# Per-head values laid out by DMA from rows in DRAM, in a fused attention and mixture-of-experts block

## The chip, the cores and the metric

The kernel runs on one core of a Trainium2 chip. The metric is the device time of one execution in microseconds, as the median of several runs. Before the change it is 536.37 us, the median of three runs (535.66, 536.37 and 537.6).

## The reference

For 4 batches of 1024 tokens of 128 features, the block normalises the tokens, runs a 16-head attention (4 heads see all earlier tokens, 12 only the last 32 and themselves) and a mixture of 16 experts of which 4 are chosen per token, and multiplies the two.

```
xn = layernorm(x)
q, k, v = split(xn @ w_qkv + b_qkv)               # 16 heads of 8 features
ctx_g = attend(q, k, v of heads 0..3,  j <= i)
ctx_l = attend(q, k, v of heads 4..15, i - 32 <= j <= i)
s = concat(ctx_g, ctx_l) @ w_out + b_out
g = silu(xn + experts(xn) + shared(xn))           # 4 of 16 experts per token, 64 wide
out = x + s * g
```

## The kernel before, in words

**Sections and order.** The work is a list of steps, walked by every engine in the same order: a first section (weights, and the preparation of batch 0), a body that is walked three times (the attention and experts of batch b, and woven into them the preparation of batch b + 1), and a last section. The order is written out by hand as strings of letters, `FIRST_ORDER`, `BODY_ORDER` and `LAST_ORDER`; `woven` takes the next step of the stream that each letter names: R the attention run, A the maxima and operands of the next heads, X the experts, P the preparation (layer norm, q, k, the first maxima), T the routing, V the values, C, 0 and 1 the context and the two output halves. Each engine's queue is strictly in this order, and a step that waits holds everything behind it on that engine. There are eight PSUM banks; two rings of three banks each (ATT, EXP) are dealt out in the order of the steps.

**Attention.** The heads come in four groups of four; groups 0, 1 and 2 of the order are local, group 3 is global. Queries and keys are kept as three half-precision planes in DRAM. For each group, SP loads strips (`qtmp`, `kall`, `("strips", g)`) and pads (`qpad`, `kpad`, `("pads", g, half)`, `("kpads", g)`), in which each of the four heads has its own 32 partitions and its own columns. `("max", g, n)` are products of `qpad` and `kall` that give each row's maximum, `("qfull", g, c)` takes the maximum off the queries and leaves them in `qall` (ACT), `("score", g, n)` are the scores, exponentiated by ACT into `prob`, and `("pv", g, n)` multiplies them with the values. SP issues the strips of group 1 only after the qall of group 0 has been copied.

**Values of the local heads.** A pv product of a local group takes as weights `vbd[:, j, group, :]`: for the block j of 32 tokens, the 128 partitions are (head, token in block), and of the 32 value columns a head's partitions hold only that head's own 8, with zeros elsewhere (the other 32 columns are the mask itself, for the sums). `("vn", c)` computes the values of 512 tokens as rows (tokens on partitions). ACT casts the local columns to the fast 32-bit format (`vn_hi`), DVE takes the rest (`vn_lo`), and four steps `("v", c, i)` multiply both with a 0/1 tile `repeat` (lines 639 and 640), which copies the 32 tokens of block i of each tile to all four heads. DVE evicts each result through a mask, `vmask`, into `vbd` (helper `tt`, line 964, called under `kind == "v"`). The global heads' values go straight to `vg` (ACT).

**Experts.** `("up", c, t)` is seven products (three for the gate, three for up, one that spreads the routing weight), then ACT, POOL (`wrow`, `hid`) and DVE, and `("down", c, t)` one product into bank 7. `("outT", c)` transposes an output half, DVE adds it to `xres`, and SP stores it.

**SP's queue around a change of batch** holds, in this order, the stores of the two output halves, the load of the next input (`xin`), the load of `xres` (which waits until both stores have landed), then strips and pads of group 1, 2 and 3.

## Time and profile before

| | before |
|---|---|
| median of 3 runs | 536.37 us |
| the profiled execution | 535.39 us, of which its span is 533.6 |
| PE matmul | 479.1 us busy, 90% of the span, 3832 instructions |
| DVE | 347.8 us, 65%, 755 instructions |
| ACT | 329.1 us, 62% |
| POOL | 269.0 us, 50% |
| SP's DMA queue | 143696 packets, 31.41 MB, 30.4% of 16 engines' span |
| mean granted TensorE clock | 0.988 |

The profile is of one execution. Durations of matmuls overlap, since they are pipelined, so that the distance between two starts is what one costs PE. "Releaser" in a wait is the instruction that ended it. An idle engine costs nothing unless it is on the chain of waits.

### The profile page before, as it was taken

The page shows a single profiled execution, that of the slowest core. Times are in us where ns is not written, and L with a number is a line of the kernel's source. Part 1 is how long each engine was busy: PE and PEld are TensorE (multiplying, and loading weights), DVE is VectorE, ACT ScalarE, POOL GpSimd, SP SyncE. Part 2 cuts the span into 40 slices and gives each one's busy share as a digit, 9 for nine tenths or more (in the row PEclk, how much of TensorE's full clock was granted, in tenths as well). Part 3 has the DMA queues.
Part 4 walks back from the last instruction along what each step waited for, and adds up shares of the span by engine and source line. Part 5 has one row for each costly group of instructions (what it writes and reads, how often), then busy time and mean ns, then how long its engine had stood idle before and what let it go on. Part 6 is the DMA issues. An engine that isn't in the chain of part 4 may idle for free.

```text
span 533.6 us, 10570 instructions
## 1 busy us (share of the span) xinstructions
PE 479.1 (90%) x3832; PEld 286.6 (54%) x3832; DVE 347.8 (65%) x755; ACT 329.1 (62%) x654; POOL 269.0 (50%) x239
## 2 busy tenths in 40 slices
PE   1859978899999989899999988999999998989995
PEld 0647554555446755555446765545546765544442
DVE  7876439775977638776787546776788532676414
ACT  3536753767956554666957556475976566366972
POOL 3407942265737852254655872145664963016623
PEclk9979999999999999999999999999999999899998
DMA  9275374000450575000350387000170178000001
GB/s 214 79 177 100 57 99 66 1 1 2 121 77 1 164 97 78 1 1 1 116 83 1 93 153 94 2 1 1 32 159 9 40 125 133 4 2 0 1 1 39
DMA packets 144077, 32.37 MB, mean 61 GB/s; under 512 B 120966, under 2 KB 136346, under 8 KB 144026
## 3 DMA queue, kind: packets, MB, share of 16 engines
q1 hardware_dynamic: 143696, 31.41, 30.4%
q8 instruction: 30, 0.49, 0.4%
q10 hardware_dynamic: 330, 0.30, 0.3%
q14 instruction: 21, 0.17, 0.1%
HBM read 22.25 MB, written 9.44 MB: 59 GB/s over the span
## 4 chain that ended last, share of the span: by engine, by line
PE 56%; DVE 13%; ACT 8%; issue 7%; SPq 6%; POOL 3%; DMA 3%; DVEq 2%; POOLq 1%; ACTq 0%
PE bank L791 8%; PE bank L739 6%; PE bank L708 5%; PE bank L678 5%; PE bank L572 4%; SPq L536 4%; PE bank L574 4%; PE bank L573 4%; PE bank L755 3%; ACT stage L936 2%; DVE mxp L1176 2%; DMA kall<-planes 2%; PE bank L646 2%; PE bank L779 2%; PE bank L715 2%
## 5 line engine op out<-in xcount | busy, mean ns | idle before, releaser
L936 ACT ACTIVATE stage<-bank 128x512 f32<-128x512 f32 (+3 forms) x240 | 112.7, 539 | 59.2 <-PE bank L712 27.9
L1253 POOL TENSOR_TENSOR wrow<-wrow,gates 128x512 f32<-128x512 f32 x64 | 82.5, 1289 | 90.6 <-ACT wrow L865 90.0
L1176 DVE TENSOR_REDUCE mxp<-bank 128x1 f32<-128x512 f32 (+4 forms) x192 | 89.8, 516 | 23.7 <-PE bank L681 14.2
L1262 POOL TENSOR_TENSOR hid<-hid,wrow 128x512 f32<-128x512 f32 x64 | 82.4, 1287 | 28.4 <-DVE hid L1140 23.5
L1245 POOL TENSOR_TENSOR maxd<-mxp,k 128x512 f16<-128x512 f32 x32 | 34.7, 1083 | 95.9 <-DVE mxp L1178 51.2
L791 PE MATMUL bank<-hid,down_w 128*128 128x512 f32 x144 | 76.0, 618 | 0.0
L1140 DVE SCALAR_TENSOR_TENSOR hid<-hid,bank 128x512 f32<-128x512 f32 x72 | 48.7, 677 | 39.5 <-PE bank L574 28.6
L854 ACT ACTIVATE hid<-bank 128x512 f32<-128x512 f32 x72 | 43.7, 606 | 44.2 <-PE bank L574 44.2
L1178 DVE TENSOR_REDUCE mxp<-bank 128x8 f32<-128x512 f32 x48 | 30.9, 686 | 49.3 <-PE bank L690 49.0
L678 PE MATMUL bank<-kall,qpad 128*128 128x512 f16 (+4 forms) x192 | 52.2, 320 | 10.6 <-DVE mxp L1176 3.7
L572 PE MATMUL bank<-xh,up_hi 128*128 128x512 f32 x144 | 58.7, 408 | 2.0 <-DVE hid L1140 1.2
L708 PE MATMUL bank<-kpad,kall 128*128 128x512 f16 (+3 forms) x192 | 55.2, 330 | 4.7 <-ACT stage L936 2.4
L574 PE MATMUL bank<-xl,up_hi 128*128 128x512 f32 x144 | 56.8, 394 | 0.0
L573 PE MATMUL bank<-xh,up_lo 128*128 128x512 f32 x144 | 56.5, 393 | 0.0
L859 ACT ACTIVATE gates<-bank 128x512 f32<-128x512 f32 x72 | 43.6, 605 | 5.8 <-POOL wrow L1253 5.8
L708 PEld LDWEIGHTS bank<-kpad,kall 128*128 128x128 f16 x192 | 17.9, 97 | 54.3 <-issue 21.5
L739 PE MATMUL bank<-stage,vg 128*32 128x512 f32 (+3 forms) x384 | 40.7, 498 | 0.0
L865 ACT ACTIVATE wrow<-bank 128x512 f32<-128x512 f32 x64 | 39.4, 616 | 0.3 <-PE bank L779 0.3
L678 PEld LDWEIGHTS bank<-kall,qpad 128*128 128x128 f16 x192 | 17.1, 97 | 37.4 <-DVE mxp L1176 16.1
L929 ACT ACTIVATE qall<-bank 128x512 f16<-128x512 f32 x32 | 18.3, 600 | 25.7 <-PE bank L663 25.6
L779 PE MATMUL bank<-cwT,pairsel 128*128 128x512 f32 x64 | 33.9, 529 | 0.3 <-issue 0.2
L572 PEld LDWEIGHTS bank<-xh,up_hi 128*128 128x128 f32 x144 | 27.1, 188 | 10.5 <-DVE hid L1140 2.5
(158 smaller groups left out, 907.7 us busy)
## 6 DMA issues: line engine op xcount, KB each, us to landing
planes<-qkh SPq DMA_DIRECT2D x16, 256.0 KB, 3.2
qtmp<-planes SPq DMA_DIRECT2D x16, 256.0 KB, 3.2
kall<-planes SPq DMA_DIRECT2D x16, 256.0 KB, 3.5
qpad<-planes SPq DMA_DIRECT2D x128, 32.0 KB, 2.8
kpad<-planes SPq DMA_DIRECT2D x48, 64.0 KB, 3.3
xin<-in_L_attn_x_dram SPq DMA_DIRECT2D x4, 512.0 KB, 4.5
planes<-qkl SPq DMA_DIRECT2D x8, 256.0 KB, 3.4
xres<-in_L_attn_x_dram SPq DMA_DIRECT2D x4, 512.0 KB, 3.7
```

The costliest lines, as they stand in the source:

```text
L572: pe.matmul(ps[:], w_hi, x_hi, start=True, stop=False)
L573: pe.matmul(ps[:], w_lo, x_hi, start=False, stop=False)
L574: return pe.matmul(ps[:], w_hi, x_lo, start=False, stop=True)
L678: ins = pe.matmul(ps[:, 0:cols], qpad[:, j, :, :], kall[:, g % 2, CH * c:CH * c + cols], start=True, stop=not last, skip_group_check=True)
L708: ins = pe.matmul(ps[:, 0:cols], kall[:, g % 2, P * j:P * (j + 1)], kpad[:, g % 2, q0 // BLK:(q0 + cols) // BLK, h, :], start=True, stop=n ...
L739: ins = pe.matmul(acc[BLK * h:BLK * (h + 1), q0 - CH * c:q0 - CH * c + cols], vg[:, j, h, :], prob[:, (SCORES_BEFORE[g] + m) % NPROB, 0:cols],
L791: pe.matmul(banks[Y][:], down_w[:, t, :], hid[:, i % NHID, :], start=(t == 0), stop=(t == NUP - 1)).then_inc(down_done, 1)
L936: act.activation(prob[:, t % NPROB, 0:cols], ps[:, 0:cols], ACT.Exp).then_inc(freed, 1)
L1140: dve.scalar_tensor_tensor(out=hid[:, i % NHID, :], in0=hid[:, i % NHID, :], scalar=1.0, in1=banks[at.bank(up)][:], op0=ALU.add, op1=ALU.m ...
L1176: ins = dve.tensor_reduce(mxp[:, c, j:j + 1], ps[:, 0:cols], AX_X, ALU.max)
L1253: pool.tensor_tensor(row, row, gates[:], ALU.mult).then_inc(gated, 1)
L1262: pool.tensor_tensor(hid[:, i % NHID, :], hid[:, i % NHID, :], wrow[:, (EP * c + t) % NWT, :] if t < EP else gates[:], ALU.mult)\
```

## The change

`vbd` is no longer computed with products. `("vn", c)` is evicted by ACT as plain 32-bit rows into a tile `vn`; SP stores these rows in a DRAM tensor `v_rows` (1024 tokens by 96 columns, two stores of 128 x 4 x 96). A single step `("v", 0)` per batch then issues twelve loads, one for each of the three local groups and four heads, which write the head's 8 columns of 32 blocks of 32 tokens to that head's 32 partitions of `vbd`. The zeros around them are written once, by POOL in the first section. The tiles `repeat`, `vn_hi` and `vn_lo`, the spreading products, the split and the masked evictions are gone. PE waits for `v_loaded` before the first pv product of a batch. The three order strings are new.

```diff
-    return [step for c in range(NCH) for step in [("vn", c)] + [("v", c, i) for i in range(4)]]
+    return [("vn", c) for c in range(NCH)] + [("v", 0)]
...
+                    elif kind == "vn":
+                        c = s[1]
+                        sp.wait_ge(emptied[at.bank(s)], at.taken(s))
+                        if at.next:
+                            sp.wait_ge(v_loaded, 16 * 4 * GLOBAL * at.next)
+                        sp.dma_start(v_rows.rearrange("(t p) d -> p t d", p=P)[:, TPC * c:TPC * (c + 1), :],
+                                     vn[:, TPC * c:TPC * (c + 1), :]).then_inc(v_stored, 16)
+                    elif kind == "v":
+                        if at.section is FIRST:
+                            sp.wait_ge(v_zeroed, 1)
+                        else:
+                            sp.wait_ge(pv_done, b * SCORES_BEFORE[HG] + SCORES_BEFORE[GLOBAL])
+                        sp.wait_ge(v_stored, 16 * NCH * (at.next + 1))
+                        for g in range(GLOBAL):
+                            for h in range(4):
+                                own = slice(HD * h, HD * (h + 1))
+                                sp.dma_start(vbd[BLK * h:BLK * (h + 1), :, g, own],
+                                             v_rows[:, BLK * g:BLK * (g + 1)][:, own].rearrange("(j k) d -> k j d", k=BLK))                                    .then_inc(v_loaded, 16)
...
-                        pe.matmul(used, repeat[:, i, :], vn_hi[:].rearrange("p t d -> p (t d)"), start=True, stop=False)
-                        done(at, s, pe.matmul(used, repeat[:, i, :], vn_lo[:].rearrange("p t d -> p (t d)"), start=False, stop=True))
...
+                        if g == 0 and n == 1:
+                            pe.wait_ge(v_loaded, 16 * 4 * GLOBAL * (b + 1))
...
-                            act.activation(vn_hi[:], tile[:, :, BLK:D], ACT.Copy)
+                            if at.next:
+                                act.wait_ge(v_stored, 16 * NCH * at.next)
+                            act.activation(vn[:, TPC * s[1]:TPC * (s[1] + 1), :], tile[:, :, BLK:D], ACT.Copy)
...
-                        elif kind == "v":
-                            c, i = s[1], s[2]
-                            tt(vbd[:].rearrange("p (t i) g c -> p i t g c", i=4)[:, i, TPC * c:TPC * (c + 1), :, 0:BLK],
-                               ps[:, 0:TPC * GLOBAL * BLK].rearrange("p (j g c) -> p j g c", j=TPC, g=GLOBAL),
-                               vmask[:, 0:GLOBAL].unsqueeze(1).broadcast_to([P, TPC, GLOBAL, BLK]), ALU.mult).then_inc(freed, 1)
...
+                    pool.memset(vbd[:, :, :, 0:BLK].rearrange("p j g c -> p (j g) c"), 0.0).then_inc(v_zeroed, 1)
```

The order strings move instructions. On SP, at the change from one batch to the next, the kernel before has (a row is a run of equal issues; `out_dram<-xres` are the stores of the output halves):

```order
L536 DMA qpad<-planes 32x16x32 x8
L546 DMA kpad<-planes 32x32x32 x4
L552 DMA out_dram<-xres 128x4x128 x2
L506 DMA xin<-in_L_attn_x_dram 128x8x128
L510 DMA xres<-in_L_attn_x_dram 128x8x128
L526 DMA qtmp<-planes 128x1024
L526 DMA kall<-planes 128x1024
```

and after the change:

```order
L537 DMA qpad<-planes 32x16x32 x8
L547 DMA kpad<-planes 32x32x32 x4
L555 DMA v_rows<-vn 128x4x96 x2
L571 DMA out_dram<-xres 128x4x128
L566 DMA vbd<-v_rows 32x32x8 x12
L571 DMA out_dram<-xres 128x4x128
L507 DMA xin<-in_L_attn_x_dram 128x8x128
L511 DMA xres<-in_L_attn_x_dram 128x8x128
L527 DMA qtmp<-planes 128x1024
L527 DMA kall<-planes 128x1024
```

The two stores of rows and the twelve loads stand ahead of the second output store and of everything behind it.

On PE, from the transposes of the first output half on, the kernel before has, in the second body pass (L779 spreads a routing weight, L572 to L574 are the experts' gate and up products, L791 a down product, L630 the value rows):

```order
L798 MATMUL bank<-k,sT 128x128 x4
L791 MATMUL bank<-hid,down_w 128x512
L639 MATMUL bank<-vn_hi,repeat 128x384
L640 MATMUL bank<-vn_lo,repeat 128x384
L630 MATMUL bank<-wv,xT 128x128 x4
L779 MATMUL bank<-cwT,pairsel 128x512
L572 MATMUL bank<-xh,up_hi 128x512
L573 MATMUL bank<-xh,up_lo 128x512
L574 MATMUL bank<-xl,up_hi 128x512
```

and after the change:

```order
L811 MATMUL bank<-k,sT 128x128 x4
L792 MATMUL bank<-cwT,pairsel 128x512
L591 MATMUL bank<-xh,up_hi 128x512
L592 MATMUL bank<-xh,up_lo 128x512
L593 MATMUL bank<-xl,up_hi 128x512
L591 MATMUL bank<-xh,up_hi 128x512
L592 MATMUL bank<-xh,up_lo 128x512
L593 MATMUL bank<-xl,up_hi 128x512
L781 MATMUL bank<-ctxT,wout 128x512
L792 MATMUL bank<-cwT,pairsel 128x512
```

The transposes of the first output half now come two expert units and one output projection (L781) earlier in the list, and both value projections lie ahead of them.

## Rows read from the trace of the kernel before

**Rows 1.** page of the profile, head and DMA packets

```profile
span 533.6 us, 10570 instructions
...
DMA packets 144077, 32.37 MB, mean 61 GB/s; under 512 B 120966, under 2 KB 136346, under 8 KB 144026
```

**Rows 2.** waits of PE from 297 to 420 us: us in total, times, longest

```profile
PE bank L678 <- issue: 1.2, 1, 1.2
```

**Rows 3.** timeline of PE around 284 to 335: start us, us, line, operands, count

```profile
295.25 0.60 PE L798 MATMUL bank<-k,sT 128*128 128x128 f32 x4
...
313.02 0.38 PE L684 MATMUL bank<-kbf 128*128 128x512 bf16 x1 [0.38 <-issue]
...
328.43 2.29 PE L755 MATMUL bank<-stage,vbd 128*64 128x64 f32 x70
331.88 0.18 PE L678 MATMUL bank<-kall,qpad 128*128 128x32 f16 x1 [1.16 <-issue]
```

**Rows 4.** timeline of SP from 295 to 345: DMA issues, start us and us

```profile
296.63 4.96 SPq L552 DMA_DIRECT2D out_dram<-xres  x2
301.64 0.51 SPq L506 DMA_DIRECT2D xin<-in_L_attn_x_dram  x1
304.88 0.38 SPq L510 DMA_DIRECT2D xres<-in_L_attn_x_dram  x1
305.94 0.34 SPq L526 DMA_DIRECT2D qtmp<-planes  x1
...
306.81 5.85 SPq L536 DMA_DIRECT2D qpad<-planes  x8
...
324.91 0.65 SPq L526 DMA_DIRECT2D qtmp<-planes  x1
```

**Rows 5.** chain of waits from 284 to 330: start us, us, what

```profile
297.06 0.89 PE bank L630 x8
...
302.15 0.17 PE bank L640
302.32 0.23 PE bank L779
...
303.94 0.86 PE bank L791 x2
...
305.27 0.61 ACT qall L929
...
316.15 4.94 DMA kall<-planes
```

**Rows 6.** instructions on tile vbd: ns min/median/max, first and last start

```profile
L964 DVE TENSOR_TENSOR vbd<-bank,k x32: 544/549/558, 41.0 to 425.6; 128x384 f32<-128x384 f32 x32
```

**Rows 7.** instructions and transfers on tile kpad, the same columns

```profile
L546 SPq DMA_DIRECT2D kpad<-planes x48: 556/664/2092, 38.8 to 446.4; - x48
...
DMA to landing us min/median/max: 2.5/3.3/4.5
```

**Rows 8.** busy time by stretch: PE, PEld, DVE, ACT, POOL, clock, DMA share, GB/s

```profile
306.00:313.00 7.00, 5.95 (x51) 3.64 (x50) 3.75 (x18) 5.21 (x11) 6.10 (x6) 1.00 0.91 179
```

**Rows 9.** timeline of POOL from 0 to 72

```profile
2.26 0.96 POOL L1199 MEMSET vg<- 128x1024 f32 x1
...
8.72 1.65 POOL L1223 TENSOR_TENSOR y<-ve,half 128x8 f32<-128x8 f32 x1 [5.08 <-DVE ve L967]
...
61.60 1.27 POOL L1262 TENSOR_TENSOR hid<-hid,wrow 128x512 f32<-128x512 f32 x1 [0.17 <-POOL wrow L1253]
```

**Rows 10.** timeline of SP from 33 to 80

```profile
42.51 0.66 SPq L506 DMA_DIRECT2D xin<-in_L_attn_x_dram  x1
...
59.62 0.34 SPq L526 DMA_DIRECT2D qtmp<-planes  x1
```

**Rows 11.** busy time by stretch around 455, columns as in rows 8

```profile
452.00:454.00 2.00, 0.72 (x12) 0.55 (x12) 0.58 (x4) 1.91 (x4) 0.00 (x0) 1.00 0.49 44
...
456.00:458.00 2.00, 2.00 (x9) 0.82 (x7) 0.84 (x3) 0.00 (x0) 0.00 (x0) 0.50 0.00 0
```

More of the change, by code:

```diff
@@ L151, in expert_steps @@
     return out
[L154 to L161 removed]
+FIRST_ORDER = ("IPIIIPPPPIIPTVTPTITPTTPVTPIIPPITIPITXIXXXXXXXXXXXIPPPPPPPIXXVX")
+BODY_ORDER = ("APAAXRAAXRRRRXPAAAXAAAAAAXRARPRAAAARAAXAAXAARXAAARRRRAAXRAAAAAAXAAARRAAARXAAAXRRARXRRXAAXAAARRRA"
+              "RAAAAAARARXRARRRARAAARAXXRRRARARAPRAARRXARRXRRRAPARAAXARRXRRXRARRRRAARAAPRPARXARXRRXPRRRRXXCRRRR"
+              "RRRTPRPPRRTTRXRRRRXXRRRXPRRRXRRPTRRRXXRRRTRTXRRRRRRRPRRRXRRRRRXCPPRPRRPRXRRRXXRRRRTRXRTPTR00XXCV"
+              "XVCX0XX11XXXV1XXXPXXXX")
+LAST_ORDER = ("AAXAXXXARRRAAAXRAAAXAAAARAXARRAARAAAARAAAAARXRRARRARXARAAAAAAAARAAAXAAAXARRRRXAAXARRAXRRRAARAAAA"
+              "XAARRAARARRARARRRRXARAAAARARAAAXRAXAAAXAAAXARXARRRRRRRRRRAXRRRRRRXRARAXRRXXRRRRXRRRRRRRRRXRRRRRR"
+              "RRRCRXCRXRRRRRXRRRRRRRXRRRXRRRRRRRRRRRRRRRRRRXRRRXRRRRXRX0XX0CXXCX0X111")
 FIRST_EXPERTS = expert_steps(0) + [("z", 0), ("z2", 0)]
@@ L238, in __init__ @@
             if s[0] in ("pv", "down", "norm", "qpads", "z", "z2", "ln", "stats", "pads", "kpads", "maxdone", "ctx", "route", "times",
-                        "mul", "strips", "setup", "fill", "ones"):
+                        "mul", "strips", "v", "setup", "fill", "ones"):
                 continue
@@ L337, in build @@
         pairsel = sb("pairsel", [P, EP, P], F32R)
-        repeat = sb("repeat", [P, 4, P], F32R)
-        vn_hi = sb("vn_hi", [P, TPC, GLOBAL * BLK], F32R)
-        vn_lo = sb("vn_lo", [P, TPC, GLOBAL * BLK], F32R)
+        vn = sb("vn", [P, NT, GLOBAL * BLK])
+        v_rows = nc.dram_tensor("v_rows", [S, GLOBAL * BLK], F32)
         half = sb("half", [P, NT])
@@ L408, in build @@
         hi_ready = sem("hi_ready")
-        vn_hi_ready = sem("vn_hi_ready")
+        v_zeroed = sem("v_zeroed")
+        v_stored = sem("v_stored")
+        v_loaded = sem("v_loaded")
         fold_ready = sem("fold_ready")
@@ L632, in walk @@
                         done(at, s, ins)
-                    elif kind == "v":
-                        c, i = s[1], s[2]
-                        if i == 0:
-                            pe.wait_ge(emptied[at.bank(("vn", c))], at.taken(("vn", c)))
-                        ps = fill(at, s)
-                        used = ps[:, 0:TPC * GLOBAL * BLK]
-                        pe.matmul(used, repeat[:, i, :], vn_hi[:].rearrange("p t d -> p (t d)"), start=True, stop=False)
-                        done(at, s, pe.matmul(used, repeat[:, i, :], vn_lo[:].rearrange("p t d -> p (t d)"), start=False, stop=True))
                     elif kind == "gate":
@@ L823, in walk @@
                             act.activation(tile[:, 0], const32(first), ACT.Copy)
-                        act.activation(repeat[:].rearrange("p i (a q) -> p i a q", a=4),
-                                       ident.rearrange("p (i q) -> p i q", i=4).unsqueeze(2).broadcast_to([P, 4, 4, BLK]), ACT.Copy)
                         act.activation(pairsel[:].rearrange("p t (e i) -> p (t e) i", e=2),
@@ L903, in walk @@
                             act.activation(vg[:, TPC * s[1]:TPC * (s[1] + 1), :, 0:HD],
-                                           tile[:, :, 0:BLK].rearrange("p t (h d) -> p t h d", d=HD), ACT.Copy).then_inc(vn_hi_ready, 1)
+                                           tile[:, :, 0:BLK].rearrange("p t (h d) -> p t h d", d=HD), ACT.Copy)\
+                                .then_inc(emptied[at.bank(s)], 1)
                         else:
@@ L1144, in walk @@
                         continue
-                    elif kind in ("weights", "small", "vbias", "vn", "v", "cwT", "max", "outT"):
+                    elif kind in ("weights", "small", "vbias", "cwT", "max", "outT"):
                         ps, freed = banks[at.bank(s)], emptied[at.bank(s)]
```

14 lines of the change are left out of this document (removed).

## Prediction, made before the changed kernel ran

> **What bounds the kernel now.** I read the page first: a span of 533.6 us [rows 1]. The second view is PE's waits over one body pass, 297 to 420 us. The longest single one is 1.2 us [rows 2], so in a pass PE nearly always has work, and whatever shortens PE's work ought to shorten the pass, unless a new wait appears. The third view says where one can appear. Take the end of one batch and the start of the next, from PE's transposes of the first output half (I call their start t0, 295.25) to the first maxima of the third group of heads at 331.88 [rows 3], 36.6 us. In the chain of waits this stretch is handed from PE to ACT's copy of qall at 305.27, and from there to SP's queue and its transfers, up to a transfer of 4.94 us that starts at 316.15 [rows 5]. The DMA timeline shows why: SP issues strips and pads for three groups of heads without a pause, the first from 305.94 and the third from 324.91 [rows 4], 19.0 us apart. The DMA engines are 0.91 busy meanwhile [rows 8]. So **in this stretch the length is SP's start plus a fixed 26.0 us** (331.88 less 305.94), and SP's start is 10.7 us after t0, set by qall.
>
> **What is taken away.** Each of the four spreading steps of a chunk is two products. Such a product stands in the chain with 0.17 us before the next one starts [rows 5]; with that rounded up a step holds PE for 0.35 us, though each product's own duration is longer because they overlap. Eight steps a batch, four batches: 32 x 0.35 = **11.2 us of PE**, 2.8 us a batch. DVE loses 32 masked evictions at 0.549 us [rows 6] and 8 subtractions of the same size, 22 us; the stretch above is not on DVE's path, so I count nothing for it. ACT's one repeat tile and one cast less are also counted at nothing, for PE starts later than the setup. If PE no longer hid DVE, the 5.5 us a batch would be a further gain, which goes into the lower end.
>
> **What is added, costed at nothing.** POOL clears 3072 elements of vbd at the start. The clear of vg, 1024 elements, took 0.96 us [rows 9], so about 2.9 us, over by 6.6 us. POOL's next work starts at 8.72 and waits for DVE [rows 9]. In the first section the twelve loads come behind the first pads, at about 43 us, ahead of the next input (42.51); strips for the next group go out only at 59.62 [rows 10], so 17 us of empty queue take them. PE's new wait for v_loaded has behind it the value products, all later maxima and experts. The loads below have landed 15 us after t0; the products that need them come some 21 us after t0. Nothing is paid unless loads take over 1 us each.
>
> **What is added and counts.** In each body pass SP now issues two row stores, one output store, twelve loads of 1024 pieces of 32 bytes, and only then the second output store, the next input, xres and the first strips. Nothing in before has 32-byte pieces. The nearest row is kpad, also 1024 pieces and 32 partitions, but of 64 bytes: median 0.664 us, shortest 0.556, longest 2.09 [rows 7]. Bounds: half of kpad by bytes, 0.33 us; above, twice qpad's 5.85/8 for 512 pieces [rows 4], 1.46 us. I take kpad's, because the number of pieces is what it shares: 12 x (0.664 + 0.04) = 8.4 us. The first of them waits until the rows have landed: stored by about t0, landing 3.3 us [rows 7], so t0 + 3. They end at t0 + 11.4, the second output store at 11.9. xres waits for its landing: now the stores' issue ends at 301.59 and xres goes at 304.88 [rows 4], 3.3 us. Then xres itself: **SP starts the strips at t0 + 15.6 instead of t0 + 10.7**, 4.9 us later. That they wait for qall no longer matters, since that is ready near t0 + 12.
>
> The Trainium skill (DMA: Bandwidth & Descriptors, Anatomy of one DMA) gives a transfer as about 2 us plus bytes over 436 GB/s, in a fit for the GpSimd path. By it a 32 KB load would occupy 0.08 us beyond its latency, all twelve 0.9 us, and the strips would still start with qall; the total would be that of the first rival. The kpad row speaks against it: 64 KB hold SP 0.664 us where the fit has 0.15.
>
> **The sum.** The stretch grows from 36.6 to 41.5 us. Its PE work changes by the order: out go five spreading steps and one value projection (5 x 0.35 + 0.89 [rows 5] = 2.6). In come two expert units (seven products at 0.23 [rows 5], 1.63 each) and one output projection (0.86, the pitch of a down product [rows 5]). Out go one down product (0.86) and one pair of value products (half of 2.29 [rows 3], 1.1). That is -2.6 + 4.1 - 2.0, about -0.4. So PE idles 4.9 + 0.4 = 5.3 us more, and the pass has 2.8 us less to do: +2.5 us, twice (first to second body pass, second to third). Into the last section the order puts 2.1 us more work in the stretch: idle grows by 2.8, against 2.8 saved: 0. The first section has no such queue. It saves 2.8, of which I give back 0.8, because POOL's products for the experts run nearly back to back near its end, one ending at 62.87 [rows 9]: -2.0. The idle is in one piece, near 6 us, at the first maxima of the second group (313.02 now [rows 3]). After PE had only 0.72 of 2.00 us busy at 452 to 454, the granted clock fell to 0.50, 1.2 GHz, by 456 [rows 11]. A fall of about 3.4 us loses 1.7 us of products; half of that lies under SP's queue: +0.85, twice. Together -2.0 + 5.0 + 0.0 + 1.7 = **+4.7 us** on the profiled execution's own time of 535.39, 540.1; the median of the runs shown, 536.37, lies 1.0 above it, so 541.
>
> **The rivals.** *Cheap loads (ends faster).* Price by bytes, 0.33 us: SP is free at t0 + 11.2, and strips start with qall at about 12.0. Against my 15.6 that is 3.6 us, three times, and no fall of the clock: 4.7 - 10.8 - 1.7 = -7.8, a median of 528.6. It decides below 0.53 us a load (4.7 / 36 less than mine). For it: the bytes are half of kpad's. Against it: qpads, half of kpad's pieces at equal piece size, cost no less than kpads in the busy stretch, 0.73 us [rows 4]. *Absorbed (no change).* While PE stands at those maxima, ACT, DVE and POOL finish the experts' backlog, so that later waits in the pass [rows 2] shrink by 1 to 2 us a pass, and the clock doesn't fall: 536 to 538. For it: POOL is nearly full before the stretch. Against it: those waits are short and few. *Dear loads (slower still).* Reading 32-byte pieces 384 bytes apart takes 1.0 us: 0.33 x 36 = 12 us more, 553; at the far bound, 1.46, it would be 569. For it: queues in this stretch are already 0.91 busy [rows 8], and the 144077 packets [rows 1] gain some 49000. *The change doesn't do what it says.* If the loads land late, the products wait at v_loaded; this is the last case again.
>
> **How the numbers follow.** Forecast (kpad's price, 538.5 to 546) 0.42; dear loads 0.13; absorbed 0.17; cheap loads 0.28. About 0.3%, 1.6 us, is what a measurement can tell from no change. So faster 0.28, same 0.17, slower 0.55. The forecast lies at 541. The range reaches to the cheap case, 528, and to 1.0 us a load, 553. The likeliest case and the dear one, of one sign, would alone give 538.5 to 553.
>
> **What would show it.** In the profile after: vbd loads near 0.66 us each on SP, a block of some 8 us between the two output stores; qtmp's issue about 15.6 us after the output transposes in body passes; a PE wait of 4 to 7 us at the first maxima of group two, on a transfer or on issue; the clock at 0.5 behind it; the first section 2 us shorter. Wrong would be: loads under 0.53 us, strips that start with qall, or a distance between two t0s that is shorter than before.

## The result, and the profile after

| | before | after |
|---|---|---|
| median of the runs made side by side | 537.01 us (535.19 to 539.09) | 540.56 us (536.74 to 544.41) |
| ratio, with its 95% interval | 1 | 1.0067 [1.0047, 1.0087] |
| span of the profiled execution | 533.6 us | 538.8 us |
| its mean granted clock of TensorE | 0.988 | 0.979 |

The change makes the kernel slower by 0.67%, 3.6 us. The forecast was 541.0, with a sum of +4.7 us. The size is right, and below it is shown that terms behind it are wrong and cancel.

The head of the page of after answers to [rows 1]:

```profile
span 538.8 us, 10462 instructions
...
DMA packets 198222, 35.53 MB, mean 66 GB/s; under 512 B 175110, under 2 KB 190490, under 8 KB 198170
```

The packets grew by 54145. The 48 loads of 1024 pieces account for 49152 and the eight stores of rows, of 512 pieces, for 4096. To see where the time went, cut the program at a piece of work that both kernels have in the same place: the first product of Qfull for the next batch. First before, then after, timeline of PE (start us, us, line, operands, count), from the second batch on:

```profile
181.85 0.38 PE L662 MATMUL bank<-qtmp,k 128*128 128x512 f16 x1
304.64 0.38 PE L662 MATMUL bank<-qtmp,k 128*128 128x512 f16 x1
427.58 0.38 PE L662 MATMUL bank<-qtmp,k 128*128 128x512 f16 x1
```

```profile
182.53 0.38 PE L673 MATMUL bank<-qtmp,k 128*128 128x512 f16 x1
308.38 0.38 PE L673 MATMUL bank<-qtmp,k 128*128 128x512 f16 x1
432.27 0.38 PE L673 MATMUL bank<-qtmp,k 128*128 128x512 f16 x1
```

At the first of these marks after is 0.7 us behind (182.53 against 181.85). The stretch to the next mark takes 125.85 us where it took 122.79 (+3.1), the one after that 123.89 for 122.94 (+0.95), and what is left of the program 106.5 for 106.0 (+0.5). Runs of one kernel differ by up to 7.7 us (table above), so of a single profiled execution the pattern counts and not the tenths: **most of the loss lies in the first of these stretches, which begins right at the first change from one body pass to the next.**

The rows of before in [rows 3] to [rows 5] are from the second such change. The timeline of SP from 292 to 332 shows the same place now and answers to [rows 4] (DMA issues: start us, us, line, tile, count):

```profile
293.85 1.28 SPq L555 DMA_DIRECT2D v_rows<-vn  x2
...
297.31 8.22 SPq L566 DMA_DIRECT2D vbd<-v_rows  x12
305.58 0.70 SPq L571 DMA_DIRECT2D out_dram<-xres  x1
306.32 0.51 SPq L507 DMA_DIRECT2D xin<-in_L_attn_x_dram  x1
308.57 0.37 SPq L511 DMA_DIRECT2D xres<-in_L_attn_x_dram  x1
309.68 0.34 SPq L527 DMA_DIRECT2D qtmp<-planes  x1
...
310.55 6.73 SPq L537 DMA_DIRECT2D qpad<-planes  x8
```

The twelve loads are there as one block of 8.22 us between the two output stores. The strips (qtmp) leave at 309.68. With t0 at 295.47 that is t0 + 14.2; before it was 10.7, and 15.6 was forecast. (The new order also puts more of PE's work behind t0 than before, so distances from t0 compare places in the program and not equal work.) Now PE over the same stretch, which answers to [rows 3], with what ended each idle time in brackets:

```profile
295.47 0.60 PE L811 MATMUL bank<-k,sT 128*128 128x128 f32 x4
...
304.23 0.51 PE L591 MATMUL bank<-xh,up_hi 128*128 128x512 f32 x1 [0.45 <-DVE hid L1154]
...
317.44 0.38 PE L695 MATMUL bank<-kbf 128*128 128x512 bf16 x1 [3.68 <-DMA qpad<-planes]
...
319.88 0.63 PE L592 MATMUL bank<-xh,up_lo 128*128 128x512 f32 x1
...
321.14 0.39 PE L592 MATMUL bank<-xh,up_lo 128*128 128x512 f32 x1
...
335.64 0.18 PE L689 MATMUL bank<-kall,qpad 128*128 128x32 f16 x1 [1.86 <-DMA qpad<-planes]
```

At 317.44 stands the wait that the forecast named, at the first maxima of the second group of heads, where before had no idle of note. It is 3.68 us here, 4.32 one pass earlier and 1.02 in the third. Behind it the same product on a 128x512 tile takes 0.63 us at 319.88 and 0.39 us again at 321.14: TensorE ran at half its clock in between. The last row is the first maximum of the third group, where the forecast's stretch ends. It stands 25.96 us behind the strips (26.0 was assumed), and 40.2 us behind t0, where before had 36.6 and 41.5 was forecast. PE waits here a second time, 1.86 us. The chain of waits of after tells on what PE stood (start us, us, what), and answers to [rows 5]:

```profile
309.01 0.61 ACT qall L943
309.68 0.34 SPq L527
...
312.07 5.12 DMA qpad<-planes
```

Two things are to be seen. **ACT's copy of qall ends when SP issues the strips**: in this pass the strips waited for qall, not for the queue. And the third pad that SP issued landed only 5.12 us later, where the median of all pads is 2.7.

The price of a load, and the clock around the two waits (stretch, its length, then busy us of PE, PEld, DVE, ACT and POOL, granted clock, DMA share, GB/s):

```profile
L566 SPq DMA_DIRECT2D vbd<-v_rows x48: 339/574/1760, 48.1 to 429.7; - x48
...
DMA to landing us min/median/max: 2.5/2.8/3.5
```

```profile
190.00:192.00 2.00, 0.00 (x0) 0.00 (x0) 1.49 (x3) 0.00 (x0) 1.83 (x3) 0.85 0.21 23
...
196.00:198.00 2.00, 2.00 (x13) 1.11 (x13) 0.00 (x0) 1.56 (x3) 1.08 (x2) 0.50 0.99 171
...
316.00:318.00 2.00, 0.56 (x9) 0.47 (x10) 1.74 (x5) 0.00 (x0) 1.26 (x1) 0.93 0.40 36
318.00:320.00 2.00, 2.00 (x17) 1.53 (x14) 2.00 (x6) 0.00 (x0) 0.00 (x0) 0.50 0.72 68
320.00:322.00 2.00, 2.00 (x13) 1.33 (x12) 0.03 (x1) 1.03 (x3) 1.05 (x1) 0.72 1.08 114
```

A load holds SP for 0.574 us in the median, and twelve of them for 8.22 us with gaps, 0.69 each; the forecast took 0.664 and a gap of 0.04. POOL's clear took 2.66 us, out of anyone's way. The clock fell to 0.50, 1.2 GHz, from about 191.4, when PE had done nothing since 187.9, and again behind the 3.68 us near 317. In before none of the windows at these places is below 1.00.

### The profile page after: what moved, and what is told of

It is laid out like the page before. It is cut to its first block, busy times and chain, and to the rows that moved or that the text cites. A ratio compares the mean times of both kernels' runs of the same rounds, so it can differ in the third digit from the quotient of the medians.

```text
span 538.8 us, 10462 instructions
## 1 busy us (share of the span) xinstructions
PE 473.5 (88%) x3768; PEld 279.5 (52%) x3768; DVE 336.8 (63%) x715; ACT 326.9 (61%) x653; POOL 269.3 (50%) x240
## 4 chain that ended last, share of the span: by engine, by line
PE 50%; DVE 17%; SPq 12%; DMA 6%; issue 5%; ACT 4%; POOL 3%; DVEq 2%; POOLq 1%; ACTq 0%
PE bank L804 7%; PE bank L750 6%; PE bank L689 5%; SPq L537 5%; DVE mxp L1181 5%; DMA qpad<-planes 4%; PE bank L719 4%; PE bank L591 4%; PE bank L593 3%; PE bank L592 3%; SPq L566 3%; PE bank L768 3%; SPq L547 2%; PE bank L792 2%; DVE cmp L978 2%
## 5 line engine op out<-in xcount | busy, mean ns | idle before, releaser
L950 ACT ACTIVATE stage<-bank 128x512 f32<-128x512 f32 (+3 forms) x240 | 110.8, 525 | 38.7 <-PE bank L723 24.6
L1251 POOL TENSOR_TENSOR maxd<-mxp,k 128x512 f16<-128x512 f32 x32 | 33.5, 1049 | 66.0 <-DVE mxp L1181 31.1
L591 PE MATMUL bank<-xh,up_hi 128*128 128x512 f32 x144 | 60.4, 419 | 1.4 <-DVE hid L1154 1.3
L689 PE MATMUL bank<-kall,qpad 128*128 128x512 f16 (+4 forms) x192 | 50.4, 319 | 12.7 <-DMA qpad<-planes 5.0
L719 PEld LDWEIGHTS bank<-kpad,kall 128*128 128x128 f16 x192 | 17.8, 97 | 47.9 <-issue 21.4
L896 ACT ACTIVATE ctxT<-bank 32x512 f32<-32x512 f32 x24 | 14.1, 587 | 33.6 <-PE bank L768 33.3
L695 PE MATMUL bank<-kbf 128*128 128x512 bf16 x48 | 19.5, 405 | 15.1 <-DMA qpad<-planes 10.9
```

Of the source, the lines that this page charges most:

```text
L591: pe.matmul(ps[:], w_hi, x_hi, start=True, stop=False)
L689: ins = pe.matmul(ps[:, 0:cols], qpad[:, j, :, :], kall[:, g % 2, CH * c:CH * c + cols], start=True, stop=not last, skip_group_check=True)
L719: ins = pe.matmul(ps[:, 0:cols], kall[:, g % 2, P * j:P * (j + 1)], kpad[:, g % 2, q0 // BLK:(q0 + cols) // BLK, h, :], start=True, stop=n ...
L950: act.activation(prob[:, t % NPROB, 0:cols], ps[:, 0:cols], ACT.Exp).then_inc(freed, 1)
```

## The experiments

Each expectation names its theories and gives their numbers. What they come down to are four questions: do the twelve loads cost what after lost; by SP's time, or by what is in flight beside them; what is the removal of the products worth by itself; and what does the new order of PE's work do. All ratios are to the kernel before, run beside them on the same chip; after and the runs below were measured on different occasions, so that a difference of two of them in us is rougher than the ratios. Diffs are against after unless said.

### Without the loads of the body passes

```diff
                         sp.wait_ge(v_stored, 16 * NCH * (at.next + 1))
+                        if at.section is not FIRST:
+                            continue
                         for g in range(GLOBAL):
```

(with both waits on v_loaded set to the count of the first section)

> The change without the twelve loads in the three body passes (the stores of the rows stay, the first section's loads stay; the local heads of batches 1 to 3 then use batch 0's values). Theory A (the forecast): the block of 8.2 to 9.4 us of loads in SP's queue is what makes PE wait at group one's first maxima; without it the time falls to 534 to 536 us, and the waits of 4.3 and 3.7 us on the pads shrink below 1.5. Theory B: in the profile after, the strips go out 14.7, 14.2 and 14.4 us after the output transposes, and the qall they wait for is ready at 13.9, since PE reaches it at 12.9 instead of the 10.9 that its own work would take; the loads cost only 0.3 to 0.8 us per pass in the queue, plus some congestion of the transfers. Then 538.5 to 540, with waits of 3 us and more at the same maxima.

Measured: 535.37 us, ratio 0.9963 [0.9936, 0.9991]. Against after's 540.56 the 36 loads of the body passes cost 5.2 us. The number is theory A's; the strips, as the rows show, are theory B's. SP's timeline in the same stretch, where t0 is 292.35:

```profile
300.97 0.50 SPq L507 DMA_DIRECT2D xin<-in_L_attn_x_dram  x1
303.34 0.38 SPq L511 DMA_DIRECT2D xres<-in_L_attn_x_dram  x1
306.58 0.34 SPq L527 DMA_DIRECT2D qtmp<-planes  x1
...
307.45 5.71 SPq L537 DMA_DIRECT2D qpad<-planes  x8
```

xres leaves at 303.34 and SP then stands idle for 3 us: the strips go at t0 + 14.2, **exactly as late as with the loads**. So in this pass the loads do not delay the strips at all. Yet PE's wait at the second group's first maxima is 2.09 us in place of 3.68 (1.15 in place of 4.32 a pass earlier). What differs is the crowd in front of the strips. In after the second output store, xin and xres leave at 305.58, 306.32 and 308.57, right before the strips at 309.68. Here xin and xres leave 5.6 and 3.2 us before them. The eight pads take SP 5.71 us here and 6.73 there, and from issue to landing they take 2.7 us in the median here and 4.3 there.

### The next residual later

If the crowd is the cause, one can thin it without touching the loads. xres (512 KB) is first needed late in the pass, and goes behind the last pads.

```diff
-                if at.section is not FIRST:
-                    for c in range(NCH):
-                        sp.wait_ge(stored[c], 16 * b + 16)
-                    sp.dma_start(xres[:], of_batch(x_v, b)).then_inc(xres_loaded, 16)
...
+                        if g == GLOBAL and half == 1:
+                            for c in range(NCH):
+                                sp.wait_ge(stored[c], 16 * b + 16)
+                            sp.dma_start(xres[:], of_batch(x_v, b)).then_inc(xres_loaded, 16)
```

> The change with the load of xres (512 KB, first needed at the pass's end) moved on SP from ahead of the first strips to behind the last pads. In the run without loads the strips go out just as late after the output transposes (14.2 us), yet their pads land 3.1 us earlier; what differs is that the second output store, xin and xres, 1.25 MB, leave SP right ahead of the strips in the change, and 5 us ahead of them without loads. Theory C: their transfers stand in the way. Then without xres between, the wait at the first maxima (4.3 and 3.7 us) falls to 2 to 3 us and the total to 536.5 to 538.5. Theory A (the issue times on SP alone): the strips are bound by qall already, nothing moves, 540 to 541.

Measured: 536.27 us, ratio 0.9978 [0.9946, 1.0009]. The wait is 1.87 us, the pads take SP 4.92 us and land in 2.9. From its timelines of SP and PE:

```profile
307.23 0.34 SPq L523 DMA_DIRECT2D qtmp<-planes  x1
...
308.08 4.92 SPq L533 DMA_DIRECT2D qpad<-planes  x8
...
331.18 0.43 SPq L539 DMA_DIRECT2D xres<-in_L_attn_x_dram  x1
```

```profile
313.18 0.38 PE L695 MATMUL bank<-kbf 128*128 128x512 bf16 x1 [1.87 <-DMA qpad<-planes]
```

All twelve loads are still there, and 4.3 of the 5.2 us are gone.

The same edit on the kernel **before** is the control: it tells what moving xres is worth where there are no loads.

> Control: the kernel before with xres's load moved behind the last pads. Its strips wait for qall and xres leaves 1 us ahead of them, so by theory C its first pads land up to 1 us earlier and the time falls by 0 to 2 us, 535 to 537; if it falls as much as the change does with the same edit, the edit is a gain of its own and says nothing of the loads.

Measured: 534.36 us, ratio 0.9949 [0.9917, 0.9981]. So the move is worth 0.51% in before and 0.89% in after (1.0067 to 0.9978). In before, too, xres leaves right ahead of the strips, at 304.88 against 305.94 [rows 4], and there, too, the eight pads behind it landed in 4.3 us in the median, and in 2.6 with xres away. The difference between the two gains, 0.38%, is no larger than their intervals, so that the cure works better with the loads than without is not shown by this pair.

The third of this set drops the body loads as well, on top of the late xres:

> The change with xres behind the last pads and without the body passes' loads. Without loads but with xres in its old place it was 535.37, with loads and xres moved 536.27. If the loads cost only through what they push against the strips (theory C), the loads cost little once xres is away: this run lies at 534 to 536. If their own 12288 pieces still cost in the queue, this run falls to 530 to 533.

Measured: 536.04 us, ratio 0.9953 [0.9925, 0.998]. With the loads it was 0.9978 [0.9946, 1.0009]: the intervals overlap, the medians are 0.2 us apart, and PE's wait is 2.02 us without loads against 1.87 with them. **Once xres is out of the way, the 36 loads cost nothing that these runs can tell.** By the ratios they cost 1.04% with xres in its place and 0.25% with it late; the difference of 0.8% is more than the four intervals together leave to chance, about 0.5%. Their 8 us of SP time lie in a stretch in which the strips wait for qall. And where xres already left 3.2 us ahead of the strips, moving it brought nothing: 535.37 with it early, 536.04 with it late, both without body loads.

### The next input ahead of the loads

```diff
                         sp.wait_ge(v_stored, 16 * NCH * (at.next + 1))
+                        if at.section is BODY and b + 2 < B:
+                            sp.wait_ge(xl_ready, NCH * (b + 1) + NCH)
+                            sp.dma_start(xin[:], of_batch(x_v, b + 2)).then_inc(x_loaded, 16)
                         for g in range(GLOBAL):
```

(with xres late, and xin at the head of the body only in its first pass)

> As the run before, and the next batch's xin is also issued ahead of the twelve loads instead of behind them (for the second and third pass). Theory C: only the second output store and xin's absence lie between loads and strips, the strips' way is free: wait at the first maxima at 1.2 to 2 us as in the run without loads, 535 to 537. Theory A: 540 to 541.

Measured: 534.93 us, ratio 0.9956 [0.9922, 0.9991]; PE's wait 1.93 us. Medians say 1.3 us better than with xres late alone, the intervals overlap: xin is not what crowds the strips, or hardly.

### The new value path in the old order

The change also replaced the three strings that order PE's work. Here they are those of before, except that the letters V stand where the new value path needs them.

```diff
-FIRST_ORDER = ("IPIIIPPPPIIPTVTPTITPTTPVTPIIPPITIPITXIXXXXXXXXXXXIPPPPPPPIXXVX")
+FIRST_ORDER = ("IPIIPPIPPIPTITPPTPTTIPITITIVIITPITXIXPXXPPPXXPVXIPVXXPPXPXXXXX")
...
```

> The new way of laying out the values in the kernel before's order (the eight spreading steps of each batch taken out of the strings, the loads where the first of the second chunk's steps stood, between the two output stores). If the new order strings are what makes the body passes wait (PE reaches the first maxima of group one 18.3 us after the output transposes, where their pads land at 19.5 even without loads), this is faster than the change: 533 to 538. If the loads and what they push together in the queue are the cause whatever the order, it lies at 539 to 543.

Measured: 560.7 us, ratio 1.0446 [1.0398, 1.0494], far outside both expected ranges. From its timelines of SP and PE, and the waits of DVE (us in total, times, longest); t0 is 306.38:

```profile
309.45 0.36 SPq L550 DMA_DIRECT2D v_rows<-vn  x1
311.62 8.03 SPq L561 DMA_DIRECT2D vbd<-v_rows  x12
...
320.53 0.51 SPq L502 DMA_DIRECT2D xin<-in_L_attn_x_dram  x1
...
323.29 0.53 SPq L522 DMA_DIRECT2D qtmp<-planes  x1
```

```profile
328.16 0.79 PE L586 MATMUL bank<-xh,up_hi 128*128 128x512 f32 x1 [8.02 <-DVE hid L1149]
```

```profile
DVE top L1075 <- DMA xin<-in_L_attn_x_dram: 26.6, 3, 9.9
```

Here the queue does rule. The rows of the second chunk are stored only 3.1 us after t0, the loads begin at t0 + 5.2, and xin behind them leaves at t0 + 14.2. In after these were t0 - 1.6, t0 + 1.8 and t0 + 10.9. DVE, whose list has the statistics of the next input at this place, stands 9.90 and 9.62 us for it at the two changes between body passes (26.6 us in all with the 7.11 of the first section; 5.8 in all in after), and PE stands behind DVE's hid, 8.29 and 8.02 us. At the third change no xin is loaded. There the strips themselves leave SP 17.8 us after t0, and PE's long idle, 7.56 us, is at the maxima. The new order brings the value projections forward, and so is no ornament of the change: without it the change would lose 23 us against before, not 3.6.

The same old order without the loads of the body passes:

> The old order with the new value path and without the body passes' loads (batches 1 to 3 then use batch 0's local values): the kernel before less its spreading products and masked evictions. This prices the removal alone. If the products held PE's path (the forecast's first term, 11.2 us of PE), the time is 525 to 528. If POOL's expert products pace PE at the change of batch (PE waited for wrow's copies there in the change, and reached qall 2.0 us later than its own work), it is 531 to 535. Against the same kernel with loads, 560.7, the difference is what the loads cost in that order.

Measured: 537.79 us, ratio 0.9997 [0.9964, 1.0029], above both expected ranges. Two readings. The loads cost 22.9 us in the old order (560.7 less 537.8), 5.2 in the new. And **the kernel without the products, with the loads of the first section alone, is no faster than before.** That isn't yet the price of the products, for the twelve loads of the first section, which this kernel keeps, are not free in the old order. Its timeline of DVE near 60 us:

```profile
65.99 1.64 DVE L1077 BATCH_NORM_STATS2 top<-xin 128x6 f32<-128x128 f32 x8 [7.08 <-DMA xin<-in_L_attn_x_dram]
```

The loads start at 53.50, xin leaves behind them at 61.60, DVE stands 7.08 us for it and PE 3.97 us for DVE, up to 69.28. At the first mark used above this kernel is 4.6 us behind before (186.41 against 181.85); from there to the end it takes 350.8 us, before 351.75. The two full body passes have no such wait. Their windows, of before and of this kernel, cut at t0:

```profile
172.50:295.25 122.75, 116.17 (x951) 69.44 (x950) 86.66 (x184) 79.64 (x159) 66.12 (x56) 1.00 0.30 59
295.25:418.20 122.95, 116.20 (x952) 69.45 (x951) 85.88 (x184) 79.64 (x159) 66.34 (x56) 1.00 0.31 59
```

```profile
177.70:300.50 122.80, 114.41 (x929) 67.35 (x935) 81.41 (x174) 79.61 (x160) 66.20 (x56) 0.99 0.32 62
300.50:421.30 120.80, 113.04 (x928) 66.69 (x934) 81.33 (x174) 79.33 (x160) 66.11 (x56) 1.00 0.33 63
```

DVE lost 5 us of work a pass, as forecast, and PE 1.8 and 3.2 us; but the passes became shorter by 0 (with a fall of the clock in it, 0.59 from 216 to 220) and by 2.15 us only. PE's idle time grew from 6.6 to 8.4 us in the first, from 6.75 to 7.8 in the second. So of 11.2 us forecast, the profiled executions show 1.0 behind the first mark. The medians leave room for more: if the 4.6 us of the start are in every execution, a whole that equals before means some 4.6 us gained behind it. **By these two readings, an estimate, the removal is worth between about 1 and 5 us here, not 11.**

### The fill of the first section one step later

```diff
-FIRST_ORDER = ("IPIIIPPPPIIPTVTPTITPTTPVTPIIPPITIPITXIXXXXXXXXXXXIPPPPPPPIXXVX")
+FIRST_ORDER = ("IPIIPPIPPIIPTVTPTITPTTPVTPIIPPITIPITXIXXXXXXXXXXXIPPPPPPPIXXVX")
```

The new order's fourth letter I puts DVE's last clearing (1.76 us) and its followers ahead of the layer norm of the first input, so that PE's first transposes wait until 14.98 us; before, they began at 12.55.

> The change with one letter moved in the first section's order: DVE's second fill (kpad, 1.76 us, and maxd, about 0.5) again comes behind the layer norm, as in the kernel before. PE's first transposes started at 12.55 us before and at 14.98 after. Theory A: the first section is a latency chain from input to the first expert, so 2.4 us come off the total: 538.1. Theory B: later steps (routing on DVE, then POOL's expert products) set the first section's end and absorb it: 540 to 540.6.

Measured: 539.49 us, ratio 1.0041 [1.0013, 1.007]. The transposes start at 12.55 again, but only 1.1 us of the 2.4 arrive in the median, and the intervals of 1.0041 and 1.0067 overlap. Inconclusive; at best half of it.

### Four loads of larger pieces

If SP's time goes by pieces, three heads' values laid side by side (pieces of 96 bytes, four loads in place of twelve) should take a third. The price is a weight tile whose columns stand 12 bytes apart.

```diff
-        vbd = sb("vbd", [P, NBLK, GLOBAL, 2 * BLK])
+        vbd = sb("vbd", [P, NBLK, 2 * BLK, GLOBAL])
...
-                            ins = pe.matmul(acc[r:r + 64, o:o + cols], vbd[:, j, HEADS[g] - 1, :], prob[:, t % NPROB, col:col + cols],
+                            ins = pe.matmul(acc[r:r + 64, o:o + cols], vbd[:, j, :, HEADS[g] - 1], prob[:, t % NPROB, col:col + cols],
```

> The change with vbd laid out with the three groups innermost, so that a head's values of all groups are one piece of 96 bytes: four loads of 1024 pieces instead of twelve of 1024 pieces of 32. PE's value products then read their weights with a stride of three elements. If a load costs by its pieces (theory A), four take 2.8 us in place of 8.2 to 9.4, and the total lies near that of the run without loads; if by bytes, they take the same 8 us and nothing moves. By theory A of the queue 534.5 to 536.5; by theory B (loads mattered little) 539 to 540. If strided weights load slower (132 to 138 ns each now), 840 of them would show it.

Measured: 545.12 us, ratio 1.0158 [1.0115, 1.0201], above both expected ranges. From the rows on tile vbd (ns min/median/max, first and last start), this kernel and then after:

```profile
L767 PEld LDWEIGHTS bank<-stage,vbd x840: 163/174/223, 73.2 to 479.7; 128*64 128x64 f32 x168
L767 PE MATMUL bank<-stage,vbd x840: 223/251/370, 73.2 to 479.7; 128*64 128x64 f32 x132, 128*64 128x32 f32 x36
L565 SPq DMA_DIRECT2D vbd<-v_rows x16: 456/647/1059, 47.8 to 429.8; - x16
```

```profile
L768 PEld LDWEIGHTS bank<-stage,vbd x840: 132/138/228, 73.2 to 472.4; 128*64 128x64 f32 x168
L768 PE MATMUL bank<-stage,vbd x840: 194/222/315, 73.2 to 472.4; 128*64 128x64 f32 x132, 128*64 128x32 f32 x36
```

The loads did what was hoped: 0.647 us for three times the bytes, 2.56 us for the four of a pass in place of 8.22. But the strided weights cost 36 ns a load and 29 ns a product, 840 times, and ACT's cast of the rows into `vn`, which now reorders the columns, 702 ns where it took 491. The products alone would be 24 us if nothing covered them. What the run shows is 4.6 us over after, and 9.8 over the kernel without body loads. A trade that loses.

### Loads later, and loads on another queue

Behind the pads of the next pass's second group, where SP's queue is otherwise full of strips and pads:

```diff
+                        if g == 1 and b:
+                            sp.wait_ge(pv_done, (b - 1) * SCORES_BEFORE[HG] + SCORES_BEFORE[GLOBAL])
+                            sp.wait_ge(v_stored, 16 * NCH * (b + 1))
...
```

> The change with the body passes' twelve loads issued behind strips, pads and kpads of group one in the next pass, not between the two output stores. Theory A: strips of group one go out with qall, PE's wait at their maxima falls from 4.3 and 3.7 us to about 3, but group two's strips come 8 us later and PE waits 6 to 8 us more there: 550 to 560. Theory B: most of the loads pass while PE has other work: 540 to 545. PE's wait for v_loaded should show as a wait on a vbd transfer at the first value products in both.

Measured: 558.1 us, ratio 1.0404 [1.0368, 1.0439]. PE's wait for v_loaded, which costs nothing in after, is now the bound: PE stands for the loads of vbd three times, 28.2 us in all and 9.9 at the longest. The number is in theory A's range, but by this wait, and not by the strips of group two that theory A named.

Issued by ACT in place of SP:

```diff
+                    if kind == "v" and at.section is not FIRST:
+                        act.wait_ge(pv_done, b * SCORES_BEFORE[HG] + SCORES_BEFORE[GLOBAL])
+                        act.wait_ge(v_stored, 16 * NCH * (at.next + 1))
...
+                                act.dma_start(vbd[BLK * h:BLK * (h + 1), :, g, own],
```

> The change with the body passes' twelve loads issued by ACT, at the place of the step in ACT's list. SP's queue then has no loads in it, and the second output store, xin and xres go out as early as without loads; but the loads' pieces run at the same time on the same DMA engines, and ACT, which works in order, is held while it issues. If a load holds ACT for the 0.57 us that it holds SP, the expert unit behind it comes 7 us late and PE waits for it: 545 to 555. If ACT only hands them over (below 0.1 us each), the time is 534 to 537.

Measured: 567.55 us, ratio 1.0537 [1.0501, 1.0572], above both expected ranges. The timeline of ACT:

```profile
311.81 11.18 ACTq L887 DMA_DIRECT2D vbd<-v_rows  x10
323.04 0.60 ACT L867 ACTIVATE hid<-bank 128x512 f32<-128x512 f32 x1 [10.98 <-issue]
```

While ACT issued these loads it did nothing else, 10.98 us, and PE waits for its wrow 8.66, 8.85 and 7.72 us at the three changes of batch. The Trainium skill (DMA: Bandwidth & Descriptors, Issuing engines are not separate DMA queues) says that issuing on several engines saves only sequencer time, "which is usually small relative to the DMA itself". The first half agrees with this run, where nothing but SP's issue time was saved. The second doesn't: the ten loads of this row held ACT 1.12 us each on average (all 36: 0.641 in the median, 2.48 the longest), against a median of 3.0 us to landing. The three waits for wrow add up to 25.2 us, nearly the 27.0 by which this run is slower than after.

### The best version

xin ahead of the loads, xres behind the last pads, and the fill one step later, together.

> The two moves that looked best together: xin ahead of the loads, xres behind the last pads, and DVE's second fill behind the layer norm in the first section. If they add up, 1 us below the run with xin and xres moved: 533 to 534.5, ahead of the kernel before, level with the kernel before with xres moved (534.36). If the first section absorbs the fill, 535.

Measured: 533.43 us, ratio 0.9931 [0.9894, 0.9968]: 7.1 us below after, and below the kernel before. Against the control, before with the late xres (534.36, ratio 0.9949), the difference is 0.9 us and the intervals overlap. So the fastest version has the change in it, but most of its gain is what moving xres gave before alone, and that the rest is real isn't shown.

## Why the prediction was right or wrong, point by point

**The price of a load: right.** Forecast 12 x 0.704 = 8.4 us, measured 8.22 in the pass shown, 9.38 and 9.23 in the others. Choosing kpad's row for its number of pieces, not its bytes, was the step that mattered, and the run with 96-byte pieces confirms it: 0.647 us for three times the bytes. (The number of pieces isn't all of it: qpad's loads, of 512 pieces, hold SP for 0.488 us in the median, not for half.) The first rival (cheap loads, 0.33 us) is false at its root.

**SP's start of the strips: wrong as a cause.** Forecast t0 + 15.6 for a queue that is late, measured 14.2 to 14.7. That the length of the stretch is SP's start plus some 26 us held (25.96 in the pass shown, 27.0 and 25.1 in the others), though it isn't fixed: without the loads it is 24.3 in all three. The failing step is the sentence that qall is ready near t0 + 12 and so "no longer matters". PE reaches Qfull at t0 + 12.9 (308.38 less 295.47), not at the 10.9 us of pure work (9.4 before, 4.1 in, 2.6 out). Two waits in front of it, 0.54 us for ACT's wrow and 0.45 for DVE's hid, are half of the difference; the other half wasn't assigned. The copy of qall that the strips wait for ends at t0 + 14.1. The kernel without loads issues its strips at t0 + 14.2 too. The queue's part was 0.6 us at the first change, 0.3 at the third and none in the pass shown, not 4.9. Strips that start with qall were one of the prediction's own signs of being wrong.

**The wait at the first maxima: right in place and near in size, by another mechanism.** Forecast one idle of nearly 6 us, or 4 to 7; measured 4.32, 3.68 and 1.02, and a second one of 1.6 to 1.9 at the third group's maxima. Of the first, 1.15 and 2.09 are there without loads in the first two passes. This part goes with the new order: PE stands at these maxima 4.1 us after the strips have left (317.44 less 3.68, less 309.68), where before it came 6.7 us after them (313.02 less 0.38, less 305.94). In before the pads of this pass landed just as late, in 4.3 us, and PE had hardly to wait for them. The rest comes from what the loads push: the second output store, xin and xres, 1.25 MB, now leave directly ahead of the strips, and the pads land late (4.3 us in the median in after, 2.7 without loads at the same start of the strips). With xres away they land in 2.9, the waits are 1.22 and 1.87 us, and what is left of the loads' cost is within the intervals.

**What is taken away: wrong.** The term of 11.2 us of PE, 2.8 a batch, did not come; between about 1 and 5 us did. The old order without body loads stands at 0.9997 of before, its first section's loads included. The pair with late xres doesn't show a gain either, 0.9953 [0.9925, 0.998] with the products removed, 0.9949 [0.9917, 0.9981] with them; but the former has the new order in it, whose waits of 1.25 and 2.02 us at the maxima and whose late start may hide one. In two body passes PE's idle time took back 1.8 and 1.0 us of the 1.8 and 3.2 that its busy time lost. The step that failed is in the first paragraph: "in a pass PE nearly always has work, and whatever shortens PE's work ought to shorten the pass". Short waits say that PE is full; they don't say that the next unit would be ready any earlier. The waits of PE in the old order without body loads show a part of it (us in total, times, longest):

```profile
PE bank L588 <- DVE hid L1151: 5.3, 3, 4.0
...
PE bank L789 <- ACT wrow L873: 2.8, 4, 0.8
```

Of the 5.3 us for hid, 4.0 are the wait in the first section told above, and the other two, 0.68 each, are nearly what before had (1.2 in total). The wait for wrow at the products that spread the routing weight wasn't there in before: 0.74 to 0.76 us at each change of batch. The rest of the idle time that grew isn't assigned. That POOL paces the experts, at 1.28 + 1.28 us a unit against 2.60 us of PE (305.78 to 308.38 in after), fits, and was in the profile; no run here slowed or sped POOL alone, so it is argued and not shown.

**The first section: wrong.** Forecast 2.0 us shorter; the first product of Qfull for the first batch comes 1.6 us later (59.59 against 57.98). From there to the first mark shown above after takes 122.9 us and before 123.9, where 2.8 us less were forecast. About 2.4 us of late start come from DVE's fill, which the order puts ahead of the first layer norm and which the forecast didn't price; moving it won back about half of that in the median, within overlapping intervals.

**The clock: right in kind.** Forecast two falls of 3.4 us each, +0.85 us each. The windows show one of over 6 us, from about 191.4 (0.85 of the window at 190) to past 198, and one of 3.4 us from 317.7. The longer one lies in the stretch that lost 3.1 us, the shorter in the one that lost 0.95. Half of the time that PE was at work in them, an estimate, is 3.0 and 1.7 us of products; how much of it lay under other waits, no run separates. The means of the profiled executions, 0.988 and 0.979, overstate the difference: the median over 77 runs of before beside the experiments is 0.978, that over after's 20 runs 0.9725.

**The rivals.** Dear loads are excluded by 0.574 us. Of the absorbed case something is seen, by another mechanism than it named: the delay by SP's queue was absorbed by PE's own late arrival at Qfull, and most of the saving by other waits. **The sum.** A pass's saving lies ahead of the mark that ends it, and the idle time behind. So by stretches, forecast against profiled execution: to the first mark shown -4.8 (the first section's -2.0 and one pass's -2.8), measured +0.7; to the second +3.35, measured +3.1; to the third +3.35, measured +0.95; from there +2.8, measured +0.5. Together +4.7 and +5.2. The missing savings and the too dear queue cancel. A reader should take the near hit as luck in the size and as right only in the sign and place.

**What stays open.** The third wait is 1.02 us where the first two are near 4. At the third change there is no next input, so 0.75 MB and not 1.25 stand ahead of the strips, and the order behind it is another; which of the two spares it was not tried. The gain of the new order alone, without the old order's trouble with xin, isn't separated from the loads: without body loads new and old order stand at 0.9963 and 0.9997 and their intervals overlap. Of the 1.25 MB ahead of the strips, xres was moved and xin was moved, the output store was not.

## What to carry to other kernels

When an edit adds transfers, look not only at the time they hold the queue but at what they push: here large transfers with plenty of time were pushed against small ones that an engine waits for, and moving a single 512 KB load behind them returned 0.9% of the time, most of what the loads had cost. Products removed from an engine that is 95% busy in a pass can bring far less than their time, here 1 to 5 us of 11, where the units behind them come from other engines; check the pitch of a unit on every engine before booking the saving. And a control on the old kernel is cheap: the cure for the new one gave the old one 0.5% too.

## What the runs showed of the hardware that was not expected

A load of 1024 pieces holds SP for about the same time at 32 bytes a piece (0.574 us, median) and at 96 (0.647); kpad's 64 bytes had 0.664 [rows 7]. Half as many pieces don't halve it: 0.488 us for qpad's 512 of 64 bytes. The Trainium skill (DMA: Bandwidth & Descriptors, Bandwidth) gives, for loads issued on the GpSimd path, a floor of 0.67 us for a small transfer of 64 packets, about 10.5 ns each; it is the time that the DMA engines are busy, not the time that the issuing queue is held. If 1024 pieces are shared evenly among 16 engines, that is an estimate of 0.67 us a load, by that page. The three rows of 1024 pieces lie within a sixth of it, while the fit by bytes on the same page, weighed in the prediction, is off by a factor of seven at 32 bytes and of three at 96. By the same count 512 pieces would take 0.34 us, and the row has 0.488.

Weights whose columns stand 12 bytes apart cost TensorE 174 ns a load where packed ones take 138, and the products behind them 251 ns where they took 222.

After 4.32 us without work, up to 192.24, the granted clock stood at 0.50 for over 6 us, and around the 3.68 us near 317 for 3.4 us, with PE at work for nearly all of both. Two waits of about the same length were followed by falls of quite different lengths.

Much of the spread between runs of one and the same kernel goes with the granted clock. Over the 77 runs of before beside the experiments its mean ranges from 0.970 to 0.989, and 0.01 less goes with 3.9 us more. A single profiled execution should be read with its own clock beside it: before's, at 0.988, is among the quickest.
